# A graph network on one core: the adjacency of a pair of tiles fetched as two transfers with a wait each

## The reference

```python
def _lightgcn_layer(x, src, dst, num_nodes):
    msgs = x[src]
    summed = jax.ops.segment_sum(msgs, dst, num_segments=num_nodes)
    ...
    return summed / denom[:, None]
...
x = _layernorm(x + _L0_gnn_ref(x, edge_index), axis=-1)          # three such layers
x = _layernorm(x + _L1_gnn_ref(x, edge_attr_64, edge_attr_2, edge_index, ...), axis=-1)
```

## Time and profile before

| What | us |
|---|---|
| median of three runs | 11443.35 |
| lowest and highest | 11409.64, 11456.6 |
| profiled execution, its own time | 11389.55 |
| its span, first to last instruction | 11387.5 |
| stretch of layers two and three within it | about 1803 to 4637 |

### The profile page before, as it was taken

The page is one execution under the profiler, slowest core; times in us unless marked ns, Lnnn a source line. Parts: engine busy times, 40 slices in busy tenths (PEclk is TensorE's granted clock), DMA queues, the critical chain, the costliest instruction groups (busy, mean ns, idle before and its releaser), DMA issues. The chain is left out here.

```text
span 11387.5 us, 219939 instructions
## 1 busy us (share of the span) xinstructions
PE 7417.4 (65%) x80448; PEld 5752.3 (51%) x80850; DVE 3539.5 (31%) x7714; ACT 3006.3 (26%) x5496; POOL 5117.5 (45%) x5109
## 2 busy tenths in 40 slices
PE   2788887766767676566666666566666666666665
PEld 1688886655656565444444444444444444444443
DVE  5777772111122222222222222222222222222222
ACT  0677772000000000122222222222222222222222
POOL 3555553444333333444444444444444444444443
PEclk6899998777877777676777777777777777777777
DMA  3333334333433333333333333333333333333332
GB/s 103 114 115 116 115 115 149 127 125 118 139 106 121 109 122 109 98 84 85 88 89 87 87 87 90 89 90 90 90 87 88 89 88 89 90 91 87 95 89 72
DMA packets 641238, 1145.18 MB, mean 101 GB/s; under 512 B 396177, under 2 KB 449533, under 8 KB 622971
## 3 DMA queue, kind: packets, MB, share of 16 engines
q0 software_dynamic: 214272, 516.37, 18.5%
q1 hardware_dynamic: 410670, 584.51, 15.5%
q10 hardware_dynamic: 15197, 28.99, 0.9%
HBM read 924.17 MB, written 205.22 MB: 99 GB/s over the span
## 5 line engine op out<-in xcount | busy, mean ns | idle before, releaser
L1765 POOL DMA_INDIRECT edge_rows<-node_table,edge_et x3224 | 3097.2, 961 | 3535.4 <-DMA edge_et<-edges_turned 2402.2
L1290 PE MATMUL two_acc<-x_parts,two_win 128*128 128x192 bf16 x16072 | 1738.4, 270 | 522.9 <-issue 503.3
L1290 PEld LDWEIGHTS two_acc<-x_parts,two_win 128*128 128x128 fp8e4 x16072 | 1530.2, 108 | 692.1 <-issue 655.8
L815 POOL DMA_INDIRECT two_rows<-x_parts,src_at x1120 | 1056.8, 944 | 1802.6 <-PE two_edge_acc L1076 1352.5
L1816 PE MATMUL edge_seg<-edge_rows,edge_sel 128*32 128x66 f32 x6448 | 1076.6, 260 | 361.6 <-issue 349.8
L1820 PE MATMUL edge_seg<-edge_rows,edge_sel 128*32 128x66 f32 x6448 | 1093.8, 262 | 306.2 <-issue 305.7
L1818 PE MATMUL edge_seg<-edge_z,edge_sel_r 128*32 128x66 f32 x6448 | 997.9, 267 | 338.6 <-issue 336.9
L1817 PE MATMUL edge_seg<-edge_rows,edge_sel 128*32 128x66 f32 x6448 | 1009.2, 266 | 290.7 <-issue 289.4
L1819 PE MATMUL edge_seg<-edge_zx,edge_sel_r 128*32 128x66 f32 x6448 | 977.4, 268 | 326.9 <-issue 325.7
L1048 ACT ACTIVATE one_win<-one_count 128x784 fp8e4<-128x784 f32 x1312 | 1066.8, 824 | 379.4 <-PE one_count L999 240.9
L1966 DVE RECIPROCAL edge_ssq<-edge_ssq 128x8 f32<-128x8 f32 x403 | 81.8, 203 | 3468.5 <-ACT edge_ssq L1874 3129.0
(11 more groups left out here) (327 smaller groups left out, 11220.5 us busy)
## 6 DMA issues: line engine op xcount, KB each, us to landing
two_win<-adjacency SPq DMA_DIRECT2D x82, 3136.0 KB
adjacency<-one_win SPq DMA_DIRECT2D x41, 3136.0 KB
edge_near<-near_ids SPq DMA_DIRECT2D x403, 192.0 KB
edge_rows<-node_table,edge_et POOLq DMA_INDIRECT x3224
node_sums<-edge_seg SPq DMA_DIRECT2D x806, 33.0 KB
two_rows<-x_parts,src_at POOLq DMA_INDIRECT x1120
edge_yd<-y_parts SPq DMA_DIRECT2D x806, 12.0 KB
node_table<-two_row SPq DMA_DIRECT2D x49, 260.0 KB
```

The costliest lines, as they stand in the source:

```text
L815: pool.indirect_dma_start(rows[:, b % 2, e, :], None, XP.rearrange("p (j c) -> (p j) c", c=3 * C), bass.IndirectOffsetOnAxis(ap=src_at[:, ...
L1290: mm = pe.matmul(acc[b][:, half * 3 * C:(half + 1) * 3 * C], win[:, b, half, j, :].bitcast(FP8), now[:, j, :], start=(j == 0), stop=(j == ...
L1765: pool.indirect_dma_start(rows[:, h.b, t, :], None, T5, bass.IndirectOffsetOnAxis(ap=et[:, h.b, 0, t:t + 1].bitcast(I32), axis=0))\
```

## The change

The load of a pair is issued as two transfers, one for each destination tile's 98 blocks, each with a semaphore of its own (`brought`, `brought2`). TensorE waits for the first ahead of its first matmul, as before, and for the second at the middle of the step, ahead of `edge_sums` and of the second tile's matmuls.

```diff
-        brought, fetched = ([sem(f"{n}{b}") for b in range(2)] for n in ("brought", "fetched"))
+        brought, brought2, fetched = ([sem(f"{n}{b}") for b in range(2)] for n in ("brought", "brought2", "fetched"))
...
                 if layer or not early(h, 2):
                     sp.wait_ge(summed, layer * DP + h.c - 1)
-                sp.dma_start(win[:, b, :, :, :].rearrange("p h j n -> p (h j n)"), A[bass.ds(h.c * P, P), :]).then_inc(brought[b], 16)
+                for half, signal in enumerate((brought[b], brought2[b])):
+                    sp.dma_start(win[:, b, half, :, :].rearrange("p j n -> p (j n)"),
+                                 A[bass.ds(h.c * P, P), half * J * P:(half + 1) * J * P]).then_inc(signal, 16)
...
                     half, j = at // J, at % J
+                    if at == J:
+                        pe.wait_ge(brought2[b], 16 * (layer * ((DP + 1 - b) // 2) + h.turn2 + 1))
+                        pe.sem_inc(issued, 1)
                     if at == J and not early(h, 1):
                         edge_sums(pe, h.back(1), sel, rows, edge_acc, sel_ready, fetched, edge_made, used, layer)
```

## The result

The changed kernel takes 11499.5 us, the kernel before 11428.2 us beside it (medians of 15 runs each, from 11448.4 to 11581.5 and from 11384.2 to 11469.2). The ratio is 1.0066, 95% interval [1.0047, 1.0085]: slower by two thirds of a per cent. The forecast was no change, with a range that ended at 11485 us, and the measured median lies above it.

What follows compares the result with a forecast made beforehand. The prediction took gathers throttling TensorE, not loads, to bound layers two and three. Its terms, minus 0.3 plus 0 plus 1 plus 0 plus 0 us, were taken as 0, giving 11443 us, range 11395 to 11485.

Steps and rivals of the forecast that it cites:

- What bounds layers two and three: Layers two and three: loader waits for its consumer, with 21 us of slack; gathers throttle TensorE, most of 503.3 us.
- The wait of the first tile: TensorE's wait for the load: 81 steps gain nothing; layer two's first starts up to 4.6 us sooner, taken as minus 0.3.
- the crawl: TensorE's last 22 matmuls of a step come in ones to threes, 0.7 us or a multiple apart, while gathers run.
- The wait and increment in the middle: New wait and increment mid-step, 82 times: 0, plus 1 us at two steps; bounds plus 7.0 and plus 2.8 us.
- a summed plus 0.7: Sum of the forecast's terms for layers two and three: minus 0.3 plus 0 plus 1 plus 0 plus 0 us.
- The second transfer on SyncE: One more 338 ns issue in 82 steps, against 21 us of slack: 0, or 28 us without that cover.
- the transfer itself: Same bytes in runs half as long, 12,544 per partition, in 82 steps: 0, any 2 us delay being within the slack.
- B: In the middle of each of 82 steps on TensorE the event costs 0.7 us: 57 or 115 us slower; chance 0.06.
- C: The mid-step wait changes TensorE's crawl; a fifth of 503.3 us of issue goes, to about 11343 us; chance 0.05.
- E: Half-length loads run slower and meet the gathers, 2 us in each of 80 steps: 160 us, 11603 us; chance 0.03.
- F: Both halves of each load share one queue and land together: no effect, 11443 us; 0.86 with Rival D and no effect.
- Rival D: Longer code shifts gaps at layers two and three's four jumps back: 15 us either way; 0.86 with F and no effect.

Runs made afterwards that it cites:

- b1: The kernel before with the load split into two transfers on one semaphore, without the middle wait; ratio 1.0019.
- b2: The kernel before with one transfer, plus a second wait and increment in the middle of each step; ratio 1.0007.
- c1: The kernel before with idle increments only, moving the edge pass's code 42 instructions on TensorE and 50 on SyncE; ratio 1.0077.
- d1: The kernel before with 42 idle increments on TensorE alone, behind layer three and ahead of the edge pass; ratio 1.0008.
- a1: The kernel before, run once more without any change; ratio 1.0005.
- c3: The kernel before with TensorE's edge-pass code moved 82 instructions by idle increments, SyncE's unmoved; ratio 1.0189.
- d2: The kernel before with 128 idle increments on TensorE alone; ratio 1.0086.
- d3: The kernel before with 256 idle increments on TensorE alone, one whole instruction block; ratio 1.0028.
- b3: The changed kernel with 20 more idle increments on TensorE, putting edge-pass code 62 (TensorE) and 50 (SyncE) instructions on; ratio 1.0092.
- c2: The kernel before with idle increments only, moving the edge pass's code 82 instructions on TensorE and 50 on SyncE; ratio 1.0134.
- c4: The changed kernel with idle increments, putting edge-pass code 82 (TensorE) and 256 (SyncE) instructions further on than in the kernel before; ratio 1.0168.
- b4: The changed kernel with 40 more idle increments on TensorE, putting edge-pass code 82 (TensorE) and 50 (SyncE) instructions on; ratio 1.0092.

## Why the prediction was wrong, step by step

*What bounds layers two and three: right.* The loader waits for its consumer still, and "issue" moved by 7 us of 503.3.

*The wait of the first tile: right.* The 81 other steps show no wait for the adjacency. In the first step TensorE began 7.1 us after the load's issue (1820.6 to 1827.7) instead of 10.95. 3.8 us of the estimated 4.6 were there, and they were gone where the crawl ends, as the step said: the free run begins 40.4 us after the issue (1860.96), before 39.9.

*The wait and increment in the middle: right in its place.* No idle time stands ahead of the 14 edge matmuls. All that the change did to layers two and three is 3.4 us in one pair of profiles, 5.6 in the other and 10 us on the average of all traces, against a summed plus 0.7 and a bound of 7.0 plus 2.8. If the average holds, the plus 1 was some 9 us too small, of the 71 that were lost.

*The second transfer on SyncE, and the transfer itself: right.* 164 issues at 352 ns, steps of layer three 37.79 us apart (37.65 before), and b1, which has both transfers, at 1.0019 [0.9992, 1.0046]. The Trainium skill, page "DMA: Bandwidth & Descriptors", section "Anatomy of one DMA", gives the fixed cost of 2.0 us, which the prediction took from it, for transfers that GpSimd issues. The loads here are issued by SyncE. The Trainium skill's rule against many small transfers names a size of 64 KB, and these are of 1568 KB. No run measures the fixed cost, and nothing in the sum hung on it.

*Rivals B, C, E and F: not seen.* b2 has B's event and stands at 1.0007; "issue" did not fall, as C would have it; the gathers take 946 ns instead of 944, where E would lengthen them; and TensorE could begin 7.1 us after the issue, when at the 326 GB/s of that stretch at most 2.3 of the pair's 3.21 MB had been moved, which F excludes.

*Rival D, the code shifts: the failed step.* It named the right cause, put it at the wrong loops and priced it by the gaps, which are not what is paid. (Its 20 to 30 instructions a body were too many as well: on TensorE a body of ten steps grew by ten.) I read the two gaps at a jump back from layer two's loop and priced them at the four jumps of layers two and three: 15 us, "inside what I call no change". There it held: the second gap moved from the 17th matmul to the 12th and shrank from 3.80 to 3.51 us. But the code behind the edit moves as well, and behind it stands a loop with some 50 turns (403 iterations by eight). D has no term for it, which puts its cost at nothing. What the runs showed in its place: everything behind layer three takes 62.7 us more in one pair of profiles and 73.1 in the other, and c1 has a ratio of 1.0077 from the displacement alone. By D's own working with 50 jumps, one gap of the earlier trace rows more per turn would have been 140 to 190 us either way. That is a case with a chance, not one inside no change, and the range would have had to reach some 11630. Even so the step would not have given the sign or the size. A second gap of 1.5 us did come up each turn, but b2 and d1 have it and lose nothing; the place that the change happened to reach costs 0.4 to 0.8 per cent, others 1.9 or nothing.

*What stays open.* Why a place costs what it costs. The second gap comes to 67 us in the changed kernel's window and goes unpunished in d1 and b2. At 82 there is almost no second gap, one fetch a turn less, and the largest loss. What decides between the two cases of the 64 matmuls, and whether the gathers slow them there, was not tried. SyncE's place changes the result by 0.5 to 0.7 per cent at both 42 and 82, in different directions, and why is open. The granted clock falls with the pace (0.72 in a1's window, 0.70 in c3's); which follows which was not tried. Padding within the edge loop, which would move its second half against its first, was not tried.

## What to carry to other kernels

An edit that adds instructions moves all code behind it, on each engine whose program grows. So price a shift by the turns of every loop behind the edit, not by those in the edited part; a measured difference of a per cent or less isn't yet the edit's own. The control is cheap: the kernel before with as many idle instructions on the same engines, and the changed kernel with as many more as fill a whole block of 256. Here the first had the loss without the edit (1.0077), and the second had the edit without most of the loss (0.9985, 1.000 and 1.0037).

## What the runs showed of the hardware that I had not expected

- 82 idle instructions on TensorE, executed once, made the kernel 1.9 per cent slower (c3), 128 made it 0.9 slower (d2), and 256 0.3 (d3), most of that their own time.
- At a jump back TensorE stood still for some 3.3 us in the edge loop, in every kernel but b3, and a second time for 1.3 to 1.5 us when the loop's head stood 42 instructions further on; at 62 (b3) the two are one stop of 6.5 us. The second stop alone made no kernel slower (d1, b2).
- A body of 2006 instructions took one fetch less per turn at 82 (399 against 457 in 6000 us), and that came with the longer turn: 134 to 136 us on average in c2, c3, c4 and b4, 131.5 in a1.
- SyncE's place was seen to count only together with TensorE's: 0/50 gives 1.0019 [0.9992, 1.0046], 42/0 1.0008, and both 1.0077.
- 64 matmuls of the edge loop took 10 to 14 us or 22 to 24 us in most turns, and the share of turns with the long case went from 5 of 45 (a1) to 21 of 44 (c3) by 82 idle instructions.
